# A two-layer transformer kernel on one core: the second pair of score products, its masks, the product with v and the output projection each move to a later slot, and the pair waits once

## The reference

```
Q, K = relu(rope(x @ wq)), relu(rope(x @ wk));  v = x @ wv
numerator   = einsum(Q, cumsum(K outer v))      # running sum over positions
denominator = einsum(Q, cumsum(K))
out = (numerator / (denominator + 1e-6)) @ wo
```

## Time and profile before

| | us |
|---|---|
| median of 3 runs | 1358.39 |
| lowest, highest | 1356.73, 1365.61 |
| profiled execution | 1368.42 |
| its span | 1366.6 |

### The profile page before, as it was taken

The page is one execution under the profiler, slowest core; times in us unless marked ns, Lnnn a source line. Parts: engine busy times, 40 slices in busy tenths (PEclk is TensorE's granted clock), DMA queues, the critical chain, the costliest instruction groups (busy, mean ns, idle before and its releaser), DMA issues. The chain is left out here.

```text
span 1366.6 us, 22165 instructions
## 1 busy us (share of the span) xinstructions
PE 1160.3 (85%) x6696; PEld 656.9 (48%) x6696; DVE 935.7 (68%) x2795; ACT 615.6 (45%) x1295; POOL 549.9 (40%) x606
## 2 busy tenths in 40 slices
PE   4999999998998999999989989898697797977720
PEld 2444343433433434434434457697576676766610
DVE  4546867868868868768758637251957869669774
ACT  1424234223223323233232247778676676777510
POOL 0000361350440550541622521545665555656564
PEclk9999999999999999999999999999798988989955
DMA  9952013013012012112139357876575656746512
GB/s 298 300 237 85 26 42 97 24 39 94 29 36 90 33 45 77 39 39 77 39 117 288 123 193 243 263 247 207 142 222 158 212 174 191 231 149 186 186 41 60
DMA packets 155288, 183.59 MB, mean 134 GB/s; under 512 B 16092, under 2 KB 103708, under 8 KB 154548
## 3 DMA queue, kind: packets, MB, share of 16 engines
q1 hardware_dynamic: 138804, 148.82, 33.8%
q0 software_dynamic: 16384, 33.59, 8.9%
HBM read 83.79 MB, written 98.57 MB: 133 GB/s over the span
## 5 line engine op out<-in xcount | busy, mean ns | idle before, releaser
L1209 POOL DMA_INDIRECT y<-y_rows,idxy x256 | 259.3, 1013 | 186.4 <-DMA y<-y_rows,idxy 97.4
L1173 POOL DMA_INDIRECT rows<-xn,idx x256 | 251.8, 983 | 88.5 <-issue 85.5
L1037 ACT ACTIVATE hs<-GY 128x512 f32<-128x512 f32 x176 | 104.9, 597 | 333.3 <-PE GY L782 333.1
L798 PE MATMUL ACC<-hs,wff 128*128 128x512 f32 x352 | 188.4, 624 | 0.0
L782 PE MATMUL GY<-xn0T,wff 128*128 128x512 f32 x352 | 186.1, 610 | 0.0
L1733 DVE SCALAR_TENSOR_TENSOR V<-y,w8all,V 128x128 f32<-128x128 f32 x232 | 82.5, 356 | 116.0 <-PE V L937 100.1
L1153 POOL TENSOR_TENSOR ppause<-neg_half 128x1 f32<-128x1 f32 x64 | 14.0, 219 | 342.3 <-DVE idx L1503 237.8
L832 PE MATMUL U<-ident,xg 128*128 128x128 f32 x576 | 98.1, 296 | 52.9 <-ACT xT L1053 46.9
L1560 DVE TENSOR_TENSOR hs<-hs,B 128x512 f32<-128x512 f32 x96 | 65.7, 684 | 65.8 <-PE B L788 35.0
L832 PEld LDWEIGHTS U<-ident,xg 128*128 128x128 f32 x576 | 69.3, 150 | 78.0 <-issue 60.2
L788 PE MATMUL B<-xw,wff 128*128 128x512 f32 (+2 forms) x304 | 102.8, 612 | 0.9 <-DVE hs L1560 0.4
(11 more groups left out here) (276 smaller groups left out, 2072.3 us busy)
## 6 DMA issues: line engine op xcount, KB each, us to landing
xg<-rows SPq DMA_DIRECT2D x144, 256.0 KB
y_rows<-ys SPq DMA_DIRECT2D x144, 256.0 KB
rows<-zero SPq DMA_DIRECT2D x2, 12288.0 KB, 47.1
rows<-zero SPq DMA_DIRECT2D x6, 2048.0 KB, 9.5
wd<-in_wd SPq DMA_DIRECT2D x1, 5120.0 KB, 24.4
wff<-in_w SPq DMA_DIRECT2D x3, 1408.0 KB, 8.9
rows<-xn,idx POOLq DMA_INDIRECT x256
y<-y_rows,idxy POOLq DMA_INDIRECT x256
```

What stands on the lines that cost most here:

```text
L798: nc.tensor.matmul(ACC[:, :], w2_0[:, v, :], hs[:, v % RH, :], start=(v == 0), stop=(v == U0 - 1))\
L1037: nc.scalar.activation(hs[:, u % RH, :], G[u % 2][:, :], ACT.Silu).then_inc(sem["silu_ready"], 1)
L1173: pool.indirect_dma_start(rows, bass.IndirectOffsetOnAxis(ap=idx[:, t * 8 + k:t * 8 + k + 1], axis=0), xn1[:, t, :], None)\
L1209: pool.indirect_dma_start(y8[:, i % RG, k, :], None, y_d[0:groups * Q * P, :], bass.IndirectOffsetOnAxis(ap=idxy[:, b, t * 8 + k:t * 8 + k ...
```

## The change

Every second pair of score products moves one slot later, with its masks and the product with v; wo moves one slot too. In the second pair, one wait for both masks takes the place of a wait ahead of each product.

```
-ATTENTION = {40: ["kp"], 41: ["cum", "outer"], 42: ["den_a"], 43: ["states", "den_b"], 85: ["oT_copy"], 86: ["wo"], 87: ["s0"]}
+ATTENTION = {40: ["kp"], 41: ["cum", "outer"], 42: ["den_a"], 43: ["states", "den_b"], 85: ["oT_copy"], 87: ["wo", "s0"]}
 for t in range(T):
     for at, name in ((32 + 2 * t, "qkv0"), (33 + 2 * t, "rope"), (45 + 10 * t, "qk_T"), (46 + 10 * t, "qkT_copy"),
-                     (49 + 10 * t, "scores_a"), (50 + 10 * t, "mask_a"), (51 + 10 * t, "scores_b"), (52 + 10 * t, "mask_b"),
-                     (54 + 10 * t, "av")):
+                     (49 + 10 * t, "scores_a"), (50 + 10 * t, "mask_a"), (52 + 10 * t, "scores_b"), (53 + 10 * t, "mask_b"),
+                     (55 + 10 * t, "av")):
...
             def s_scores_b(t):

-                pe.wait_ge(*seen.next("at_ready"))
+                pe.wait_ge(*seen.next("at_ready", 2))
                 score_now(2, "X0")
-                pe.wait_ge(*seen.next("at_ready"))
                 score_now(3, "X1")
```

## The result

| | before | changed |
|---|---|---|
| median of 22 executions each, us | 1365.63 (1356.73 to 1373.55) | 1359.02 (1347.58 to 1365.27) |
| profiled execution, us (span) | 1368.42 (1366.6) | 1356.72 (1354.9) |
| mean granted clock in it | 0.942 | 0.941 |

The ratio is 0.9952 by the two medians; by the comparison of the executions it is 0.9959, 95% interval 0.9941 to 0.9977. The change makes the kernel faster, by 0.2 to 0.6%. I had forecast 1348.3 and a range up to 1358.0: the measured time lies 1.0 beyond it.

What follows compares the result with a forecast made beforehand. The prediction took PE to bound the first layer until about 796 us. Tiles 6.3, back edges 1.4 and seam 2.4 summed to 10.1 us, taking the median from 1358.4 to 1348.3, range 1340 to 1358.

Steps and rivals of the forecast that it cites:

- Tile 0: First layer, second score pair: no more wait for the second mask, less an extra narrow/full change; 0.30 saved a batch.
- Tile 2: First layer, down product, gate product and score pair: done sooner without PE standing before each score product; 0.95 saved a batch.
- Tile 1: First layer: masks now behind topk0b make PE's product with v wait; about 0.35 lost a batch.
- Back edges: Loop's jump after batches 2 to 5: PE's stop for xn0T shrinks; 1.4 saved in all, low bound 0.
- another reading: Loop's jump: if PE's sequencer runs 64 ahead, its jump is hidden; the term would be 2.0, the sum 10.7.
- Seam: End of batch 7: weight load issued earlier, so the last scatter group lands sooner; first second-layer rows 2.4 sooner, bounds 0 and 3.0.
- The sum: Whole kernel: tiles 7 x (0.30 + 0.95 - 0.35) = 6.3, loop ends 1.4, end of batch 7 2.4; 10.1 us saved.
- The other reading: Tile 0's extra tiling change: if a drain pays a product's whole recorded tail, the sum is 7 x 0.07 = 0.5 smaller.
- The second layer keeps its order, and I let it move as a block: Second layer: assumed to shift as a whole, so the first layer's saving reaches the end in full.
- rival C: Gain stops at a bound: ends give nothing or second-layer transfer waits take it back; 1354 to 1359; chance 0.18.
- The base: Starting time from which the saving was subtracted: the median of the runs, 1358.4.
- rival D: Slower: tile 1's masks behind topk0b stop PE over 1.25 a batch, up to 2.23; 1365.3 less the ends' gain; chance 0.05.

Runs made afterwards that it cites:

- rep_before: The kernel before run once more, no edit: 1364.93 us.
- rep_after: The changed kernel run once more, no edit: 1358.17 us, ratio 0.9942 to the kernel before.
- first_before: The kernel before with the second layer left out: 808.65 us.
- first_after: The changed kernel with the second layer left out: 798.82 us.
- cut_before2: The kernel before without GpSimd's last 64 gathers, repeated on a chip at full clock in the first layer: 1344.85 us, ratio 0.9864 to the kernel before.
- cut_after2: The changed kernel without GpSimd's last 64 gathers, repeated: 1340.97 us, ratio 0.9836 to the kernel before.
- both: The changed kernel with topk0b behind tile 1's masks and weight load part 6 issued one step into the second layer: 1357.09 us, ratio 0.9912 to the kernel before.
- block_behind: The changed kernel with topk0b one slot later, behind tile 1's masks: 1355.05 us, ratio 0.9927 to the kernel before.
- slots_only2: The changed kernel's new slots with the old two waits, on a slower chip: 1470.24 us against 1475.04 for the kernel before.

## Why the prediction was wrong

Point by point, against its own steps.

- **Tile 0, gain 0.30**: measured 0.30.
- **Tile 2, gain 0.95**: measured 0.90. The small stop before the pair is 0.13, as forecast; 0.05 more goes elsewhere in the tile.
- **Tile 1, loss 0.35**: measured 0.37 to 0.45, mean 0.42, released by the masks behind topk0b as said. In batch 7, which has no topk0b, the distance is the old 11.12.
- **Back edges, 1.4**: measured 2.0, and 2.2 to 2.6 in the other pairs of profiles (rep_before and rep_after, first_before and first_after, cut_before2 and cut_after2). I had allowed for PE's own jump and let 0.25 a time be left; nothing is left. (The 0.47 at the end of batch 6 is scatter: in the repeats it is -0.13.) Beside it I had set another reading: with the queue depth of 64 that the Trainium skill gives for TensorE (TensorE: Matmul & The Clock Gate, section Architectural detail) the jump would be hidden and the four edges bring 2.0. The trace agrees with a hidden jump: four stops of 0.39 to 0.49 vanish, and the four have 2.00 less in their distances. PE has 2.67 of work from wo to the product that used to wait (397.44 to 400.11), as the rows show; the depth of 64 no run shows.
- **Seam, 2.4**: measured 2.1, and 1.5 in the repeats; both shows that the load causes the long landing. That it hits the group is not certain: in cut_before2, whose first layer is that of before, the group escaped it.
- **The sum, 10.1**: the traces give 10.18 and, in the repeats, 9.07; the first layer by itself 9.83. The tile terms were 0.9 too high in sum, the back edges 0.6 too low, and 0.7 of the 10.18 is scatter, so that the sum met it so closely is in part luck. The other reading that I had set beside tile 0, after the Trainium skill's TensorEngine Tiling (Array Packing), section Tiling Modes, would have made its gain 0.23; the trace's 0.30 goes with the rows.
- **"The second layer keeps its order, and I let it move as a block"**: this step failed. The order is kept, but of the 9.8 that the first layer saves by itself only 6.4 reach the end: 3.4, give or take 2.2, are lost, and not through the last gathers, since without them 5.9 are (give or take 2.5). That was part of rival C (the second layer takes back what comes sooner), to which I had given 0.18 with all of its losses together. I had named its waits for transfers as the cause; the executions point at the granted clock, which I had read as 1.00 in the loop and then left out of the argument, though in the second layer it is 0.91 to 0.94 up to the tail. How the loss comes about stays open: the clock explains about half of it, by correlation.
- **The base**: I set the sum against the median of the three executions shown, 1358.4. Of 22 the median is 1365.6, and on other chips 1363 to 1367: three executions that scatter over 15 to 20 us lay 7 low. With the right base the same sum gives 1355.5, inside my range, and the measured 1359.0 is 3.5 above it.

So two steps failed. The absolute miss of 10.7 is 7.2 of the base and 3.5 of the gain, and of these 3.5 some 3.2 belong to the block step. That the profiled execution came out at 1356.72, near the 1358.3 that I had for it, is luck: that pair of executions differs by 11.7, the repeats by 7.4. The sign, the size within 1% of no change, and the mechanism in the first layer are right; rival D (tile 1's stop over 1.25) is refuted by 0.42, and B's 13.7 by the topk0b stop, which block_behind shows to be worth some 3 by itself.

## What to carry to other kernels

A merged wait saves nothing by itself: what helps is to put the consumer a slot later, where both of its inputs are there, and then to look at what else has moved ahead of the producer on its engine (topk0b here). A gain in one stage is worth its full size in that stage alone; measure the stage by itself, and don't take it for granted that a later stage moves as a block. On a chip where the same program is slower, look for waits that the other chips don't have before laying it to the clock. And three executions of a kernel that scatters by 15 us are no base for a prediction of 10: widen the range by the base's own uncertainty.

## What the runs showed of the hardware

The same program takes 1365 us on three chips and 1473 on two. In the first layer of the kernel before 44 us of the difference arise, 26.0 of them with PE standing still, mostly behind late starts of ACT that no profile from the other chips shows, and 18.4 with longer products, the granted clock falling to 0.93 over 100 us where it is 1.00 on the others. A gain of 0.5% on the first kind is none on the second. The scatter of 8 to 20 us of the whole kernel is 1 us in the first layer and 5 us without GpSimd's last gathers. A change of the loop's batch leaves DVE idle for 2.4 us and PE not at all where PE has 2.67 us of work at that place. A scatter group beside which a 768 KB load is issued lands in 2.8 to 5.3 us instead of 2.23, in eight profiles 4.0 to 5.3 after the load's issue. Two score products behind one wait take 1.06 together, and 1.19 in tile 2 of slots_only2, with a wait ahead of each.
